# Experts' results added to one array in HBM by adding indirect DMAs, instead of written six times a token and summed at the end

## What is computed

```python
scores = softmax(x @ gate_w.T)                     # 64 experts
topk_w, topk_ids = top_k(scores, 6); topk_w /= sum(topk_w) + 1e-20
...
routed = einsum('tef,ehf->th', silu(g) * u * comb[:, :, None], w_down)
shared = (silu(sg) * su) @ ws_down.T               # two shared experts
return routed + shared
```

## Time and profile before

| | |
|---|---|
| time, median of 3 runs | 1550.52 us (1549.78 to 1550.93) |
| span of the profiled execution, first to last instruction | 1551.0 us |
| own time of the profiled execution beside its span | none given |
| mean granted clock of TensorE, share of full speed | 0.926 |
| busy over the span | PE 1296.3 us (84%), DVE 1096.4 (71%), ACT 841.7 (54%), POOL 685.7 (44%) |
| first and last indirect DMA of `experts` start | 1175.8 and 1473.8 us |
| first load of `results` is issued | 1476.05 us |

### The profile page before, as it was taken

The page is one execution under the profiler, slowest core; times in us unless marked ns, Lnnn a source line. Parts: engine busy times, 40 slices in busy tenths (PEclk is TensorE's granted clock), DMA queues, the critical chain, the costliest instruction groups (busy, mean ns, idle before and its releaser), DMA issues. The chain is left out here.

```text
span 1551.0 us, 29748 instructions
## 1 busy us (share of the span) xinstructions
PE 1296.3 (84%) x8828; PEld 1136.6 (73%) x8828; DVE 1096.4 (71%) x2210; ACT 841.7 (54%) x1859; POOL 685.7 (44%) x584
## 2 busy tenths in 40 slices
PE   5899899899899899999899897549809999999800
PEld 3788788788788788788788786536408888888700
DVE  3686776686776676786776777552109999999778
ACT  2565565465565465565565554711107888888701
POOL 3443433443433343543433420057745777777600
PEclk9999999999999999999999999569959999999955
DMA  6320040120140120040300000032237887888574
GB/s 218 94 70 2 29 142 15 41 70 2 32 139 14 42 70 1 21 148 4 112 1 1 1 1 31 1 72 103 104 109 233 242 239 238 239 239 236 173 248 131
DMA packets 100315, 151.51 MB, mean 98 GB/s; under 512 B 10410, under 2 KB 73038, under 8 KB 100196
## 3 DMA queue, kind: packets, MB, share of 16 engines
q1 hardware_dynamic: 89156, 124.75, 26.9%
q0 software_dynamic: 11040, 25.30, 4.8%
HBM read 92.51 MB, written 62.46 MB: 100 GB/s over the span
## 5 line engine op out<-in xcount | busy, mean ns | idle before, releaser
L461 DVE TENSOR_REDUCE neg_max<-scores 128x1 f32<-128x256 f32 (+7 forms) x256 | 192.6, 753 | 196.5 <-PE scores L571 196.5
L379 ACT ACTIVATE pt_hi<-pt 128x512 fp32r<-128x512 f32 (+3 forms) x384 | 174.5, 489 | 245.2 <-PE pt L580 243.6
L429 DVE TENSOR_TENSOR pt_lo<-pt,pt_hi 128x512 fp32r<-128x512 f32 (+3 forms) x384 | 201.3, 552 | 28.5 <-ACT pt_hi L379 12.1
L500 PE MATMUL o_ps<-pt_hi,v_hi 128*128 128x256 f32 (+1 forms) x640 | 196.6, 307 | 21.1 <-DVE o_lo L437 18.5
L356 ACT ACTIVATE probs<-scores,neg_max 128x256 f32<-128x256 f32 (+7 forms) x256 | 189.8, 742 | 43.3 <-DVE neg_max L461 29.9
L318 POOL TENSOR_TENSOR turned<-taken,cos 128x512 f32<-128x512 f32 x80 | 108.1, 1352 | 177.0 <-ACT taken L366 176.8
L580 PE MATMUL pt<-ident,probs 128*128 128x128 f32 x1152 | 171.0, 276 | 16.5 <-DVE pt_lo L429 14.9
L501 PE MATMUL o_ps<-pt_lo,v_hi 128*128 128x256 f32 (+1 forms) x640 | 181.4, 284 | 0.0
L502 PE MATMUL o_ps<-pt_hi,v_lo 128*128 128x256 f32 (+1 forms) x640 | 181.0, 283 | 0.0
L1061 POOL DMA_INDIRECT results_dram<-y_sb,dest x134 | 149.3, 1114 | 35.5 <-issue 30.0
L310 POOL TENSOR_TENSOR q_lo<-turned,q_hi 128x512 fp32r<-128x512 f32 x64 | 83.2, 1299 | 183.9 <-ACT q_hi L389 183.9
(11 more groups left out here) (186 smaller groups left out, 3698.3 us busy)
## 6 DMA issues: line engine op xcount, KB each, us to landing
rows_dram<-empty SPq DMA_DIRECT2D x32, 919.1 KB
up_raw<-in_up SPq DMA_DIRECT2D x69, 368.0 KB, 3.8
x_in<-rows_dram SPq DMA_DIRECT2D x68, 258.0 KB, 3.3
parts<-results_dram SPq DMA_DIRECT2D x16, 768.0 KB, 9.5
down_raw<-in_down SPq DMA_DIRECT2D x69, 128.0 KB, 2.7
down_raw<-in_down_tail SPq DMA_DIRECT2D x69, 112.0 KB, 3.5
w_raw<-in_w SPq DMA_DIRECT2D x8, 768.0 KB, 8.6
x_raw<-in_xT SPq DMA_DIRECT2D x8, 512.0 KB, 4.5
```

Source lines behind the costliest of these rows:

```text
L379: nc.scalar.activation(pt_hi[m // 2 % 2][:, a:z, P * (m % 2):P * (m % 2) + P], pt_ps[c % 2][:, 0:P * (z - a)].rearrange("p (k q) -> p k q" ...
L429: nc.vector.tensor_tensor(pt_lo[m // 2 % 2][part], pt_ps[c % 2][:, 0:P * (z - a)].rearrange("p (k q) -> p k q", q=P), pt_hi[m // 2 % 2][pa ...
L461: nc.vector.tensor_reduce(neg_max[:, n % 4:n % 4 + 1], scores_ps[n % 2][:, 0:key_tiles(n) * P], AX.X, ALU.max, negate=True).then_inc(max_m ...
L500: nc.tensor.matmul(out, lh, rh, start=first, stop=False)
```

## The change

The results are added up in HBM. A new array `sums` has one row a token and 256 spare rows. At the end of `routing` SP writes `resid` (residual and shared experts) to it. Each indirect DMA of `send` has the operation add: it reads the rows at its destinations, adds its own and writes them. In POOL's loop `landed(n - 1)` now stands before `send(n)`. An unfilled row no longer has a destination out of bounds: DVE takes the smaller of its destination and a spare row's number, so all 128 rows of each DMA are carried out. At the end SP loads `sums` in four groups of four tiles into `resid`; the sum of six and the addition are gone, and statistics are taken on the loaded rows.

```diff
@@ routing, SP @@
+            sp.wait_ge(added, done(T // BLK - 1))
+            sp.dma_start(dram["sums"][0:T, :].rearrange("(i p) c -> p i c", p=P), resid[:]).then_inc(sums_begun, 16)
+            sp.dma_start(dram["sums"][T:T + SPARE, :].rearrange("(i p) c -> p i c", p=P), resid[:, 0:SPARE // P, :]).then_inc(sums_begun, 16)
             sp.wait_ge(table_in, 16)
+            sp.wait_ge(sums_begun, 32)
@@ routing, POOL: the row number sent with a token @@
-            pool.iota(goes_with[:, :, :, 0], [[P, TILES], [T, WAYS]], base=0, channel_multiplier=1,
+            pool.iota(goes_with[:, :, :, 0], [[P, TILES], [0, WAYS]], base=0, channel_multiplier=1,
@@ experts, SP @@
             sp.wait_ge(all_sent, 1)
-            for t in range(TILES):
-                if t >= RING:
-                    sp.wait_ge(parts_used, t - RING + 1)
-                sp.dma_start(parts[t % RING][:], results[t]).then_inc(parts_in[t % RING], 16)
-                if t >= 2 * GROUP_TILES and t % GROUP_TILES == 0:
-                    store(sp, t // GROUP_TILES - 2)
-            store(sp, TILES // GROUP_TILES - 2)
-            store(sp, TILES // GROUP_TILES - 1)
+            for g in range(GROUPS):
+                tiles = slice(g * GROUP_TILES, (g + 1) * GROUP_TILES)
+                sp.dma_start(resid[:, tiles, :], sums[:, tiles, :]).then_inc(sums_in[g], 16)
+            for g in range(GROUPS):
+                store(sp, g)
@@ experts, POOL @@
                     pool.indirect_dma_start(
-                        out=dram["results"], out_offset=bass.IndirectOffsetOnAxis(ap=dest[buf][:, s:s + 1], axis=0),
+                        out=dram["sums"], out_offset=bass.IndirectOffsetOnAxis(ap=dest[buf][:, s:s + 1], axis=0),
                         in_=y_sb[buf][:, s, :], in_offset=None, bounds_check=last_row,
-                        oob_is_err=False).then_inc(y_out[buf], 16)
+                        oob_is_err=True, compute_op=ALU.add).then_inc(y_out[buf], 16)
+            pool.iota(spare[:], [[P, SUB]], base=T, channel_multiplier=1, allow_small_or_imprecise_dtypes=True).then_inc(spare_made, 1)
                 for u in range(-2, 1):
                     split_up(i, u + 4)
+                    landed(i, u - 1)
                     send(i, u)
-                    landed(i, u - 1)
@@ experts, DVE @@
-                dve.tensor_copy(dest[buf][:], goes_with[buf][:, :, 0])
+                dve.tensor_tensor(dest[buf][:], goes_with[buf][:, :, 0], spare[:], ALU.min)
-            for t in range(TILES):
-                dve.wait_ge(parts_in[t % RING], 16 * (t // RING + 1))
-                dve.tensor_reduce(total[:, t % 2, :], parts[t % RING][:].rearrange("p j c -> p c j"), AX.X,
-                                  ALU.add).then_inc(parts_used, 1)
-                dve.wait_ge(parts_used, t + 1)
-                then(dve.tensor_tensor(resid[:, t, :], resid[:, t, :], total[:, t % 2, :], ALU.add))
-                then(dve.bn_stats(stats[:, t, :], resid[:, t, :]))
-                then(dve.bn_aggr(moments[:, t, :], stats[:, t, :]))
+            for g in range(GROUPS):
+                tiles = slice(g * GROUP_TILES, (g + 1) * GROUP_TILES)
+                dve.wait_ge(sums_in[g], 16)
+                for t in range(g * GROUP_TILES, (g + 1) * GROUP_TILES):
+                    ins = dve.bn_stats(stats[:, t, :], resid[:, t, :])
+                then(ins)
+                for t in range(g * GROUP_TILES, (g + 1) * GROUP_TILES):
+                    ins = dve.bn_aggr(moments[:, t, :], stats[:, t, :])
+                then(ins)
```

More of the change, by code:

```diff
@@ L45 @@
 WAYS = TOPK
+SPARE = 256
 TAIL = FFN - P
@@ L670, in routing @@
         gated, silu_made, hidden_made = sem("shared_gated"), sem("shared_silu_made"), sem("shared_hidden_made")
-        downed, added = sem("shared_downed"), sem("shared_added")
+        downed, added, sums_begun = sem("shared_downed"), sem("shared_added"), sem("sums_begun")
         block = ctx.enter_context(nc.Block())
@@ L958, in experts @@
         goes_with = three("goes_with", [P, SUB, 2])
-        RING, GROUP_TILES = 8, 4
-        parts = [sb(f"parts{i}", [P, WAYS, H]) for i in range(RING)]
-        total = sb("total", [P, 2, H])
+        GROUP_TILES = 4
+        GROUPS = TILES // GROUP_TILES
+        spare = sb("spare", [P, SUB])
         stats, moments = sb("stats2", [P, TILES, 6]), sb("moments2", [P, TILES, 2])
@@ L979, in experts @@
         send_begun, all_sent = sem("send_begun"), sem("all_sent")
-        parts_in = [sem(f"parts_in{i}") for i in range(RING)]
-        parts_used, dve_step = sem("parts_used"), sem("dve_step2")
+        sums_in = [sem(f"sums_in{g}") for g in range(GROUPS)]
+        spare_made, dve_step = sem("spare_made"), sem("dve_step2")
         variance_made, deviation_made, normed, out_done = sem("variance_made"), sem("deviation_made"), sem("normed2"), sem("out_done")
@@ L985, in experts @@
         row_blocks = dram["rows"].rearrange("(n p s) c -> n p s c", p=P, s=SUB)
-        results = dram["results"].rearrange("(j i p) c -> i p j c", j=WAYS, p=P)
+        sums = dram["sums"][0:T, :].rearrange("(i p) c -> p i c", p=P)
         out_tiles = out.rearrange("b (i p) c -> (b i) p c", p=P)
@@ L1032, in _ @@
             sp.wait_ge(all_sent, 1)
-            for t in range(TILES):
-                if t >= RING:
-                    sp.wait_ge(parts_used, t - RING + 1)
-                sp.dma_start(parts[t % RING][:], results[t]).then_inc(parts_in[t % RING], 16)
-                if t >= 2 * GROUP_TILES and t % GROUP_TILES == 0:
-                    store(sp, t // GROUP_TILES - 2)
-            store(sp, TILES // GROUP_TILES - 2)
-            store(sp, TILES // GROUP_TILES - 1)
-            sp.wait_ge(out_done, 16 * (TILES // GROUP_TILES))
+            for g in range(GROUPS):
[3 more added lines that the diff above has]
+                store(sp, g)
+            sp.wait_ge(out_done, 16 * GROUPS)
         @block.gpsimd
@@ L1046, in _ @@
             pool.sem_inc(y_sent, 3)
-            last_row = pool.to_reg(WAYS * T - 1)
+            last_row = pool.to_reg(T + SPARE - 1)
             def split_up(i, u):
@@ L1082, in _ @@
                     split_up(i, u + 4)
+                    landed(i, u - 1)
                     send(i, u)
-                    landed(i, u - 1)
             split_up(triples, 2)
             for u in range(-2, 1):
+                landed(triples, u - 1)
                 send(triples, u)
-                landed(triples, u - 1)
             landed(triples, 0)
@@ L1179, in _ @@
             dve.sem_inc(hidden_split, 3)
+            dve.wait_ge(spare_made, 1)
             def x_lower(i, u):
@@ L1265, in scales @@
                                          op0=ALU.mult, op1=ALU.mult).then_inc(scales_made, 1)
-            for t in range(TILES):
-                dve.wait_ge(parts_in[t % RING], 16 * (t // RING + 1))
-                dve.tensor_reduce(total[:, t % 2, :], parts[t % RING][:].rearrange("p j c -> p c j"), AX.X,
-                                  ALU.add).then_inc(parts_used, 1)
-                dve.wait_ge(parts_used, t + 1)
-                then(dve.tensor_tensor(resid[:, t, :], resid[:, t, :], total[:, t % 2, :], ALU.add))
-                then(dve.bn_stats(stats[:, t, :], resid[:, t, :]))
-                then(dve.bn_aggr(moments[:, t, :], stats[:, t, :]))
[L1275 to L1279, removed]
+            for g in range(GROUPS):
[7 more added lines that the diff above has]
+                then(ins)
+                dve.tensor_scalar(deviation[:, tiles], moments[:, tiles, 1], EPS_LN, None, ALU.add).then_inc(variance_made, 1)
+                if g > 0:
                     scales(g - 1)
-            scales(TILES // GROUP_TILES - 1)
+            scales(GROUPS - 1)
         @block.tensor
@@ L1398 @@
     dram["rows"] = nc.dram_tensor("rows_dram", (ROWS, ROW), F32, kind="Internal").ap()
-    dram["results"] = nc.dram_tensor("results_dram", (WAYS * T, H), F32, kind="Internal").ap()
+    dram["sums"] = nc.dram_tensor("sums_dram", (T + SPARE, H), F32, kind="Internal").ap()
     dram["table"] = nc.dram_tensor("table_dram", (P + 1, 1), I32, kind="Internal").ap()
```

## The result

The changed kernel takes 1701.88 us (median of 4 runs, 1701.43 to 1703.14) against 1550.63 before in the same comparison: a ratio of 1.0975, 95% interval 1.096 to 1.0991. It is 151 us slower. Its profiled execution has a span of 1699.7 us.

What follows compares the result with a forecast made beforehand. The prediction took PE to bound the blocks (4.50 us each) and DVE the tail. Profiled span 1551.0 - 50.2 (tail) + 153.1 (blocks) + 1.2 (last landing) + 0.1 (iota) = 1655.2 us, forecast 1655, range 1550 to 1790.

Steps and rivals of the forecast that it cites:

- the circle: POOL's blocks: first send, second send, its landing, then the steps to the next start; at least L + 2.22 us a block.
- the forecast of 2.3 us a block: PE in the blocks: waiting behind POOL and DVE, it gets a gap of some 2.3 us a block.
- The landing: Second send of a block: plain part 3.4 us, plus 1.2 for adding, two thirds of a 64 KB load's 1.8.
- L: Landing time of a block's second send in POOL's loop: 4.6 us, ends 3.1 and 6.5, break-even 3.04.
- the 6.82: Predicted length of a block in us, instead of 4.50; over 66 steps +153.1 us.
- The distance: POOL's loop: time from a block's first send to its second, taken as 1.48 us.
- the way back: POOL's loop: from a wait's end to the start of the send that waited, taken as 0.74 us.
- The tail: Behind the blocks, bound by DVE: from 74.95 us to 24.7 from the first load's issue, a gain of 50.2.
- The small edits: Writing `sums` nothing (11 us if uncovered), one iota 0.1, DVE's minimum nothing, last landing 1.2 more.
- Landings as on empty queues: Rival in the blocks: adding DMAs land in 2.4 us, block 4.62, kernel 1509 us; chance 0.10.
- Row after row at the price of the 4-byte writes: Rival in the blocks: reading, adding and writing row by row, landing 9.2 us, block 11.42, kernel 1965 us; chance 0.10.
- The clock: Rival in the blocks: PE with gaps is granted 0.50, a block needs 7.9 us, kernel 1727 us; chance 0.12.

Runs made afterwards that it cites:

- The wait alone: Kernel before with only `landed(n - 1)` moved ahead of `send(n)`, sends still plain writes to `results`: 1698.84 against 1619.12 us, +79.7.
- the add alone: Kernel before with only the operation add on its sends to zero-filled `results`, wait still behind the sends: 1684.03 against 1619.12 us, +64.9.
- three arrays: Changed kernel with block n adding to sums array n modulo 3 and the wait back behind the sends: 1584.56 against 1553.38 us for the kernel before.
- The run with more work for PE: Changed kernel with each block's transposes done four times on PE: 1714.58 against 1553.38 us for the kernel before, +161 instead of +151.

## Why the prediction was right, and where its sizes were off

**What bounds the kernel, and the circle.** Right. PE bounded the blocks, and with the wait ahead of the sends POOL's circle does. The wait alone and the add alone were each shown to cost, and three arrays, which allow the wait to go back behind the sends, return 120 us. PE's long gaps are not one a block, as the forecast of 2.3 us a block reads, but 4.3 us once in three blocks.

**The landing.** Plain part 3.4, measured 3.48 and 3.56; the adding 1.2, measured 1.1; L = 4.6, measured 4.65. For the adding this is in part luck. The prediction reasoned that every landing takes 1.2 us more, two thirds of a load's 1.8; the trace has 0.4 more in two blocks of three and 2.5 more in the third, beside the loads of two blocks. Nothing in the prediction stands for these long landings, and no run shows what causes them. In the short blocks L was 0.6 too high, which made up for what the next terms were too low, and so these blocks, 6.6 to 7.0 us, are near the 6.82.

**The distance and the way back.** These are the terms that were mis-sized: "first send, second send 1.48 us later" and "from the end of `y_sb` to the start of the send that waited for it are 0.74 us". The first was taken from plain sends; no row showed an adding one, and this term was given no bound from above, though the landing was. It is 1.93. The way back is 0.94, because `landed`'s own steps stand ahead of the 0.74. 0.45 of distance, 0.20 of way back and 0.05 of landing make 0.70 of the 0.74 us by which a block was missed; over 66 steps that is 49 us. The rest nearly cancels: the tail is 3.3 us shorter than forecast, the first send 2.6 us earlier, the last landing and the last distance 1.1 longer, and a run's time is 1.7 us above its span in the changed kernel (1701.43 and 1699.7), where the prediction took the span for the time. So 1655 became 1702.

**The tail.** Predicted 24.7 us and a gain of 50.2, measured 21.4 and 53.5. The load took 3.9 (4.0 predicted); DVE did a group in 2.0 us instead of 2.8, since statistics overlap (1.42 for four, 0.39 for the aggregation).

**The small edits.** Writing `sums` cost nothing where POOL's sending ended last. In the other comparisons the cover was gone, and it cost 8.5 us, where the prediction had set 11 against that case. The last landing grew by 1.7 us (3.74 against 2.07), not 1.2.

**Rivals.** Landings as on empty queues: no; they are 4.65 us, and no landing of the changed kernel is below 3.7. Row after row at the price of the 4-byte writes: no, 9.2 us was not reached (largest landing 6.5). The clock: it did fall, to 0.82, which is one of the prediction's own signs of being wrong, and 1702 lies nearer to this rival's 1727 than to 1655, so the time alone would not have decided between them. The run with more work for PE does: while POOL's circle sets the block, neither 1.8 us more work nor a clock of 0.92 moves it by more than 0.1 us. In the three arrays, where POOL's floor is only a little above PE's 4.50 us, gaps and clock together cost 0.3 us a block.

The fixed cost plus bytes that the Trainium skill gives (DMA: Bandwidth & Descriptors, section Anatomy of one DMA), an estimate of 2.3 us for such a send, agrees with the unhidden plain landings of 2.07 and 2.4 us. It agrees neither with those beside SP's loads nor with any of the adding ones.

## What to carry to other kernels

A wait for a DMA's landing ahead of the next DMA makes a circle, and its price is not the landing alone: add the issuing of everything between, and the steps from the wait to the next start. Ask of an operation that is new to the trace how long it takes to issue as well as to land. If the order is needed only because two DMAs may meet in one place, give them separate places before giving them a wait.

## What was not expected of the hardware

An indirect DMA of 128 rows is issued in 1.6 us when it adds, and in 1.0 to 1.2 when it writes; it is the same with 28% of its rows left out.

POOL's `split_up` reads 0.97 us alone and 1.55 when it follows an adding send at once; it starts inside that send's record.

In the comparisons in which the kernel before took 1619 to 1622 us, PE's matmuls for the shared experts stand 2.8 us apart while POOL sends rows, waiting for nothing that the profile shows (start, us, instruction, idle before; the changed kernel):

```profile
1065.74 0.58 PE L922 MATMUL places_ps<-shared_down,shared_hidden 128*128 128x256 f32 x1 [2.21 <-issue]
1068.55 0.58 PE L923 MATMUL places_ps<-shared_down,shared_hidden 48*128 48x256 f32 x1 [2.22 <-issue]
```

PE is busy 16 of 80 us from 1060 to 1140, and 65 of 72 from 1140 on, when the sending has ended; in the first comparison it was busy 81 of 82 us beside the same sends. Why some comparisons have this and others don't stays open.

The landings of adding DMAs in the chain fall into two groups, 3.7 to 4.5 and 5.5 to 6.5 us, with nothing between, while plain ones with the same wait stay below 4.6. Most of the long ones stand beside the loads of two blocks; in the three arrays, with a DMA share of 0.90, the median of all landings is 5.1 us (3.8 to 6.3). No run moved these loads, so that they are the cause is not shown.
